# Counting the support of a sparsemax row: three halving adds and sums replaced by one long sum per tile

## What is computed

```python
zs = -jnp.sort(-x, axis=-1)
cssv = jnp.cumsum(zs, axis=-1) - 1.0
support = zs > cssv / rho
k = jnp.maximum(jnp.sum(support, axis=-1, keepdims=True), 1)
tau = jnp.take_along_axis(cssv, k - 1, axis=-1) / k
return jnp.clip(x - tau, 0.0)
```

## Time and profile before

| | |
|---|---|
| profiled execution, own time | 985.46 us |
| its span, first to last instruction | 983.7 us |
| mean granted TensorE clock | 0.943 of full speed |
| median of three other runs | 986.68 us |
| instructions | 14681 |

### The profile page before, as it was taken

One profiled execution on the slowest core, in us unless ns is written; L12 is line 12 of the kernel. 1 busy time (PEld: TensorE's weight loads), 2 busy tenths in 40 slices (PEclk: granted clock), 3 DMA queues, 4 the chain that ended last, 5 costly groups with the idle time before them and its releaser, 6 DMA issues.

```text
span 983.7 us, 14681 instructions
## 1 busy us (share of the span) xinstructions
PE 830.8 (84%) x4960; PEld 686.6 (70%) x4960; DVE 768.8 (78%) x1972; ACT 634.3 (64%) x914; POOL 503.7 (51%) x348
## 2 busy tenths in 40 slices
PE   2250748999998989999999989898999999889998
PEld 1130537777787878777777878787887877767887
DVE  1679687989989898989898998989898979854221
ACT  1565575867687776768676867777686767563221
POOL 3455644656555665646465555666463656523010
PEclk9765558999999999999999999999999999999999
DMA  7100001010201001010102020010101010101010
GB/s 242 47 1 14 0 11 48 11 58 1 68 2 54 15 12 58 11 58 13 57 1 69 1 68 1 17 53 12 58 12 58 1 55 1 54 1 54 1 54 11
DMA packets 16182, 33.58 MB, mean 34 GB/s; under 512 B 1980, under 2 KB 12905, under 8 KB 14057
## 3 DMA queue, kind: packets, MB, share of 16 engines
q1 hardware_dynamic: 13760, 27.61, 9.0%
q0 software_dynamic: 1248, 4.73, 1.4%
q10 hardware_dynamic: 1096, 0.29, 0.2%
HBM read 28.30 MB, written 4.33 MB: 33 GB/s over the span
## 4 chain that ended last, share of the span: by engine, by line
PE 38%; DVE 33%; issue 11%; ACT 9%; POOL 6%; DMA 2%; ACTq 0%; DVEq 0%; POOLq 0%
PE y_ps L711 12%; PE h_ps L698 8%; PE s_ps L655 6%; DVE fsum L825 5%; PE m_ps L663 5%; ACT signs L448 4%; DVE g L968 4%; DVE fold_a L822 4%; DVE asum L856 4%; PE m_ps L671 3%; DVE first L939 3%; PE m_ps L614 3%; POOL over L306 3%; DVE fold_b L829 2%; ACT hid L494 2%
## 5 line engine op out<-in xcount | busy, mean ns | idle before, releaser
L306 POOL TENSOR_TENSOR over<-S,tau 128x1232 f32<-128x1232 f32 x128 | 285.8, 2248 | 189.1 <-DVE tau L841 186.4
L711 PE MATMUL y_ps<-w_sb,hid 128*128 128x256 f32 x1152 | 281.2, 388 | 47.1 <-ACT hid L494 42.7
L711 PEld LDWEIGHTS y_ps<-w_sb,hid 128*128 128x128 f32 x1152 | 214.4, 191 | 94.2 <-ACT hid L494 63.7
L698 PE MATMUL h_ps<-x1nT,w_sb 128*128 128x256 f32 x1152 | 277.3, 385 | 0.0
L698 PEld LDWEIGHTS h_ps<-x1nT,w_sb 128*128 128x128 f32 x1152 | 216.7, 192 | 30.0 <-issue 3.0
L825 DVE TENSOR_REDUCE fsum<-over 128x16 f32<-128x1232 f32 x128 | 183.2, 1431 | 27.9 <-ACT over L450 27.9
L448 ACT ACTIVATE signs<-over 128x1232 bf16<-128x1232 f32 x128 | 156.1, 1220 | 14.7 <-POOL over L306 14.7
L450 ACT ACTIVATE over<-over 128x1232 f32<-128x1232 f32 x128 | 157.5, 1231 | 4.1
L822 DVE TENSOR_TENSOR fold_a<-signs 128x640 bf16<-128x640 bf16 x128 | 99.4, 777 | 63.5 <-ACT signs L448 63.5
L494 ACT ACTIVATE hid<-g 128x512 f32<-128x512 f32 x144 | 89.8, 624 | 89.0 <-DVE g L968 88.5
L968 DVE SCALAR_TENSOR_TENSOR g<-h_ps,sw_all 128x512 f32<-128x512 f32 x128 | 87.4, 684 | 55.4 <-PE h_ps L698 39.6
(11 more groups left out here) (93 smaller groups left out, 934.4 us busy)
## 6 DMA issues: line engine op xcount, KB each, us to landing
sw_all<-sw_scratch SPq DMA_DIRECT2D x16, 1024.0 KB, 5.2
x_sb<-in_x SPq DMA_DIRECT2D x16, 256.0 KB, 2.6
w_sb<-in_w POOLq DMA_DIRECT2D x2, 2048.0 KB, 12.0
out_y<-y SPq DMA_DIRECT2D x16, 256.0 KB, 5.5
ctx_sb<-in_ctx SPq DMA_DIRECT2D x16, 77.0 KB
wk_sb<-in_wk SPq DMA_DIRECT2D x1, 256.0 KB
wv_sb<-in_wv SPq DMA_DIRECT2D x1, 256.0 KB
wq_sb<-in_wq SPq DMA_DIRECT2D x1, 256.0 KB
```

The lines of the kernel that those rows point to most:

```text
L306: return pool.tensor_tensor(dst, S[:, p, t], tau[:, p, t].rearrange("p (h o) -> p h o", o=1).broadcast_to([P, NH, NK]), ALU.subtract)
L698: last = pe.matmul(h_ps[:, i % 2, c, :], w1_sb[:, e, k, c * P:(c + 1) * P], x1nT[:, p, k, :], start=(k == 0), stop=(k == KC - 1))
L711: last = pe.matmul(y_ps[:, t, :], hid[:, i % 2, c, t * P:(t + 1) * P], w2_sb[:, e, c, :], start=(i == 0 and t == 0 and c == 0), stop=(i == ...
```

## The change

The two folds and the sum of the second go. In their place each tile's signs, 16 rows of 80 bf16 values, are summed by one tensor_reduce straight into that tile's half of den, at the place where fold_a stood. So a round has two long sums of signs in place of two fold_a, one fold_b and one short sum. Nothing of the count stands behind `between()` any more: the reciprocal is the first instruction there. Two of the four steps of `newton_chain` go, and the step computation now also waits for the second fsum. The signal that frees the signs has a new name and comes from the new sum.

```diff
-        fold_a, fold_b = sb("fold_a", [P, T, NH, SW // 2], BF16), sb("fold_b", [P, T * NH, SW // 4], BF16)
...
-        f_summed, signs_folded = sig("f_summed", ROUNDS * T), sig("signs_folded", ROUNDS * T)
+        f_summed, signs_summed = sig("f_summed", ROUNDS * T), sig("signs_summed", ROUNDS * T)
...
-        newton_chain = sig("newton_chain", 4 * ROUNDS)
+        newton_chain = sig("newton_chain", 2 * ROUNDS)
...
-                n0 = 4 * r
+                n0 = 2 * r
                 for t in range(T):
                     dve.wait_ge(sign_done.sem, sign_done.at(b, rt(r, t)))
-                    dve.tensor_tensor(fold_a[:, t], signs[:, p, t, :, 0:SW // 2], signs[:, p, t, :, SW // 2:], ALU.add
-                                      ).then_inc(signs_folded.sem, 1)
+                    dve.tensor_reduce(den[:, p, t * NH:(t + 1) * NH], signs[:, p, t], AX.X, ALU.add
+                                      ).then_inc(signs_summed.sem, 1)
                     dve.wait_ge(relu_done.sem, relu_done.at(b, rt(r, t)))
                     dve.tensor_reduce(fsum[:, t * NH:(t + 1) * NH], over[:, p, t], AX.X, ALU.add
                                       ).then_inc(f_summed.sem, 1)
-                dve.wait_ge(signs_folded.sem, signs_folded.at(b, rt(r, 1)))
-                halves = fold_a[:].rearrange("p t h k -> p (t h) k")
-                dve.tensor_tensor(fold_b[:], halves[:, :, 0:SW // 4], halves[:, :, SW // 4:], ALU.add
-                                  ).then_inc(newton_chain.sem, 1)
                 between()
+                dve.wait_ge(signs_summed.sem, signs_summed.at(b, rt(r, 1)))
+                dve.reciprocal(rden[:], den[:, p]).then_inc(newton_chain.sem, 1)
+                dve.wait_ge(f_summed.sem, f_summed.at(b, rt(r, 1)))
                 dve.wait_ge(newton_chain.sem, newton_chain.at(b, n0 + 1))
-                dve.tensor_reduce(den[:, p], fold_b[:], AX.X, ALU.add).then_inc(newton_chain.sem, 1)
-                dve.wait_ge(newton_chain.sem, newton_chain.at(b, n0 + 2))
-                dve.reciprocal(rden[:], den[:, p]).then_inc(newton_chain.sem, 1)
-                dve.wait_ge(newton_chain.sem, newton_chain.at(b, n0 + 3))
                 dve.scalar_tensor_tensor(step[:], fsum[:], -1.0, rden[:], ALU.add, ALU.mult
                                          ).then_inc(newton_chain.sem, 1)
-                dve.wait_ge(newton_chain.sem, newton_chain.at(b, n0 + 4))
+                dve.wait_ge(newton_chain.sem, newton_chain.at(b, n0 + 2))
```

More of the change, by code:

```diff
@@ L444, in sign_relu @@
                 if r:
-                    act.wait_ge(signs_folded.sem, signs_folded.at(b, rt(r - 1, t)))
+                    act.wait_ge(signs_summed.sem, signs_summed.at(b, rt(r - 1, t)))
                 else:
-                    act.wait_ge(signs_folded.sem, signs_folded.at(b - 2))
+                    act.wait_ge(signs_summed.sem, signs_summed.at(b - 2))
                 act.activation(signs[:, p, t, :, 0:NK], over[:, p, t], ACT.Sign).then_inc(sign_done.sem, 1)
```

## The result

The changed kernel takes 990.91 us (median of 20 runs, 987.94 to 995.04), the kernel before beside it 986.9 us (20 runs, 985.33 to 988.71). The ratio is 1.0043, with a 95% interval of 1.003 to 1.0055: slower by 0.43%, as forecast in sign and nearly in size (+4.0 us between the medians, +5.0 predicted). The profiled execution took 990.21 us with a span of 988.4 us, against 985.46 and 983.7.

A forecast was written before the change was run, and what follows sets the result against it. No engine is full; the bound is a chain through TensorE, ACT and VectorE repeating every 53.72 us. Steady turns 13.7 - 2.7, turn 16 +0.1, first turns -6.1: +5.0 us on 986.68, so 991.7 us, range 983 to 998.

The forecast's parts named there:

- The turn: Steady mid-run period of the chain, 53.72 us before: the four rounds together add 0.93 us, giving about 54.6 us.
- The price of the sum: VectorE's new sum of 1280 bf16 values: 1.48 us long, 1.40 us on the chain, bounds 1.35 and 1.51.
- The rival of held sums: GpSimd stretches the new sums on VectorE as it does the folds: 1011 us; 4%.
- the draw by a cheap sum: The new sum costs only 1.35 to 1.37 us on the chain: 987.5 to 989 us; 23%.
- Round 1, +1.14: Ahead of the verdict's cast: two sums, 2.80 us, replace 1.66 us of folds, uncovered because TensorE already waits.
- Round 2, +0.10: Paced by ACT's signs up to gate 2: sums only partly hide in relu waits, fold_b's 0.40 pays nearly all.
- Round 0, -0.31: On VectorE's own stretch, wholly on the chain: 3.11 us of folds and den go, 2.80 us of sums come.
- Round 3, 0: Beside TensorE's 15.7 us stretch: tau comes 0.75 us earlier, but VectorE waits for the projection, so no gain.
- The first turns, -6.1: Start of the run, GpSimd waiting for tau: unstretched rounds gain 2.15 and 2.43 us, about 1.5 more ahead.
- The prediction's own sign: In the first turns: a gain under 4 us would mean GpSimd's subtractions were not what stretched the folds.
- The whole: Whole run: 13.7 - 2.7 + 0.1 - 6.1 = +5.0 us, giving 991.7 us.
- The faster rival: Round 3's earlier tau reaches the chain through TensorE's second norm, 0.75 us in each of 13 turns: 982 us; 15%.

The follow-up runs named there:

- sum in round 1 alone: Kernel before with the single long sum per tile in round 1 only, from batch 2 on, old folds elsewhere: 1002.13 us, ratio 1.015.
- the experiment: Kernel before with single sums in all rounds of batches 0 and 1 only, old folds in all others: 983.28 us, ratio 0.9952.
- sum in round 3 alone: Kernel before with the single long sum per tile in round 3 only, from batch 2 on, old folds elsewhere: 977.96 us, ratio 0.9909.
- folds in round 1: Changed kernel with the old folds back in round 1 of every batch, single sums in rounds 0, 2 and 3: 988.04 us, ratio 1.0006.
- early verdict: Changed kernel with round 1's verdict cast moved between the two tiles' sums instead of behind all four: 988.43 us, ratio 1.0005.
- without fold_b: Kernel before with fold_b removed and den summed from fold_a behind the gate or verdict: 998.07 us, ratio 1.01.
- folds in round 3: Changed kernel with the old folds back in round 3, from batch 2 on: 992.07 us, ratio 1.0057.
- sums in rounds 0 and 2: Kernel before with single sums in rounds 0 and 2 and all of batches 0 and 1, folds elsewhere: 978.71 us, ratio 0.993.

## Why the prediction was right, point by point

**The turn.** Read between the same instructions of both chains (the earlier trace rows and above), its parts are: from the first layer 2 to that behind gate 2, 12.75 us instead of 12.68 (+0.07); TensorE's stretch, 15.73 both times; from x to the first sum of round 1, 20.45 instead of 20.74 (-0.29); round 1 up to layer 2, 5.68 instead of 4.57 (+1.11). That is +0.89, where the prediction had 0.10, 0, -0.31 and 1.14, together +0.93. This part was right step by step.

**The price of the sum** (1.40 on the chain, 1.48 long): measured 1.39 and 1.478, and never held. The busy time of the new sums, expected at 189.4 in place of 188.0, was 189.2. The rival of held sums is out, and so is the draw by a cheap sum.

**Round 1, +1.14**: TensorE's wait for the cast went from 0.26 to 1.38 us a turn, +1.12, and the sum in round 1 alone makes the turn 1.12 longer.

**Round 2, +0.10**: from the sign at 544.36 to gate 2 at 549.84, 5.48 against 5.40 before: +0.08.

**Round 0, -0.31**: -0.29 between the chains. By experiment, rounds 0 and 2 together give -0.21 to -0.36; expected -0.21.

**Round 3, 0**: right in number, wrong in reason. I held that 0.75 us of earlier tau was covered by TensorE's stretch. With folds in round 0 it is worth 0.79 a turn; in the changed kernel it is worth nothing because the sums of round 0 do not wait for GpSimd. What I booked under round 0 as "1.48 of fold_a goes" was this wait. The hold goes once and was booked once, so for the whole change the sum was right. For round 3 taken alone it was wrong by 0.7 to 0.8 us a turn, as the expectation for that run was.

**The first turns, -6.1**: against the kernel before, the two taus came 1.4 and 3.5 us earlier, not 4 and 6. The two rounds themselves took 6.14 and 6.45 us, so they gained 2.17 and 2.14 of the 2.15 and 2.43 that were forecast. What failed to come is the 1.5 us ahead of them: the first sum starts at 73.02 instead of 72.23. Some 1.4 us of the gap comes from ahead of all Newton rounds: the scores at 26 us took TensorE 2.84 us instead of 1.63, in this execution, and the first tau is 1.4 us late by it and by the second tile. Such scores take 2.81 us at the low clock (at 107.87 us of the same trace), but the clock row of the profile reads 1.00 at 26 us, so the cause is not shown. No sum of signs stands ahead of them, so it is hardly the change. The prediction's own sign, under 4 us gained would clear GpSimd's subtractions, thus misleads: the second tau came only 3.5 us earlier, but the held folds (2.32 and 2.54 us) became sums of 1.48. By the experiment the first turns give 4.4 to 6.2 us.

**The whole.** By verdicts, the profiled execution is 2.9 us ahead at turn 4 (5.2 by the prediction's terms), loses 13.4 up to turn 16 (11.2), and gains 5.8 from there to the end (1.0): +4.7 in the span, predicted +5.0. Of the 13.4, 2.1 us are the three turns at low clock, which I had not foreseen. Of the 5.8, some 4 us have nothing to do with the price of the sums: in the kernel before, TensorE ran at the low clock behind 867 and 911 us with its matmuls on the chain, and one small transfer took 2.09 us instead of 1.28. The changed kernel has a low stretch at 867 us too, but ahead of its layer 2 at 877.32. So misses of 2.3 and 2.2 us one way and of 4.8 us the other cancelled. That the total came within 1 us was luck; that a turn grows by 0.9 us was not.

**The faster rival** (tau of round 3 reaches the chain) was given 15% and a price of 9.8 us, by way of the second norm. The price was near (977.96 against 986.21 with the sum in round 3 alone, 8.3 us) and the way was wrong: it is the fold of round 0, not the norm. The changed kernel can't have that gain, since the same edit takes away the folds that were held.

## What to carry to other kernels

An instruction that is far longer on the chain than its median, like the fold of 1.56 us against 0.49, may be a wait without a name; look at what the other engine runs at its end, and follow the chain there. A hidden piece of work is priced by the slack of its cover, and here that was a quarter of a microsecond (0.22 us at x, 0.26 at the verdict), so a change should be applied where it pays and not everywhere: here the long sum belongs in the round whose tau is waited for, and the folds where little may stand ahead of a hand-over. And when an edit lets TensorE run ahead, look at its longest idle in each turn and at the granted clock behind it before believing the gain.

## What was not expected of the hardware

TensorE's clock fell to 1.2 GHz in runs where it is busy for 92 to 94% of the middle (200 to 853 us) and hardly ever idles longer than 1.93 us (once 2.18). Ahead of the last layer 2 of a turn, three kernels idle for 1.92 us in all thirteen steady turns, but for the one of 2.18. Their traces have 3 (changed kernel), 8 (folds in round 1) and 11 (early verdict) low stretches there. So the long idle does not bring the low clock by itself. In the ten other traces the idle is mostly 1.37 to 1.79 us, 1.78 in every turn without fold_b, and there is one low stretch in all of them together. It stands behind the one idle of 1.92 us in the run with folds in round 3; a turn with 1.92 in another run and one with 1.88 in a third kept the full clock.

What else decides is open, but the traces have a hint. In the three kernels with 1.92 us, the low stretches start 54.61 us apart, or twice that, although their undisturbed turns take 54.61, 53.50 and 53.31 us. In the changed kernel, whose turn is as long as this distance, the last ten turns all kept the full clock. So it may count at what moment of time the idle falls, and the changed kernel may have more or fewer such turns from one execution to the next. No run varies this alone.

What a low stretch costs also varies with where it falls: the turns it touches are 0.2 to 2.6 us longer than undisturbed ones. Over the eleven turns from 207 to 808 us with folds in round 1 it comes to 1.5 us for each of the eight stretches. The changed kernel's runs spread over 7.1 us and those before over 3.4, and the number of such turns may be part of it. But the run with folds in round 3 has one of them in its trace and spread over 5.3 us, and that with sums in rounds 0 and 2 has none and spread over 5.9, so this stays open.
